# Gated two-layer transformer step on one core: register loads in batches, a twelve-place ring, later attention norms, and block results scaled on ScalarE

## The reference

```python
x = x + tanh(g_xattn[0]) * conv_mixer(layernorm(x), k, bias, ctx)      # filters over time, 8 heads
x = x + tanh(g_ffn[0])   * moe0(layernorm(x))                         # below
x = x + tanh(g_xattn[1]) * causal_attention(layernorm(x), ctx, ctx)   # 16 heads of 16 channels
x = x + tanh(g_ffn[1])   * lora_moe(layernorm(x))                     # 704 hidden, rank 16, 8 experts

def moe0(x):                                                          # E=8 experts, top 2, F=176
    probs = softmax(x @ Wr); w, sel = top_k(probs, 2)
    C = sum_k w[:, k] * one_hot(sel[:, k], E)
    routed = sum_e C[:, e] * ((silu(x @ Wg[e]) * (x @ Wu[e])) @ Wd[e])
    shared = (silu(x @ Sg) * (x @ Su)) @ Sd                           # 704 hidden
    return routed + sigmoid(x @ Wsg) * shared
```

## Time and profile before

| | us |
|---|---|
| median of 3 runs | 894.62 |
| lowest, highest | 890.34, 896.23 |
| the profiled execution, whole | 894.95 |
| its span, first to last instruction | 893.2 |

### The profile page before, as it was taken

How to read it: one execution, slowest core, us unless ns; L and a number is a source line. 1 busy time by engine, 2 the same in 40 slices (tenths; PEclk the granted TensorE clock), 3 DMA queues, 4 the chain that set the end, 5 groups by cost and what they waited for, 6 DMA issues and landing times.

```text
span 893.2 us, 13171 instructions
## 1 busy us (share of the span) xinstructions
PE 724.9 (81%) x4198; PEld 574.7 (64%) x4214; DVE 577.9 (65%) x1221; ACT 309.4 (35%) x539; POOL 256.0 (29%) x256
## 2 busy tenths in 40 slices
PE   2788888587978778877874888997769899999995
PEld 2565666476767656656662555665658788788884
DVE  5879888472356444444353778889457976877764
ACT  2110110154422222222232566875334335334231
POOL 1979777454447000000076810100100000000000
PEclk9999999797979899999995789998679999999997
DMA  8210100132213222222165512120010101001000
GB/s 271 71 50 27 36 24 1 48 95 74 70 56 140 67 78 68 73 73 77 42 110 98 81 50 82 54 85 2 1 47 1 48 25 48 1 24 48 23 1 24
DMA packets 42923, 51.25 MB, mean 57 GB/s; under 512 B 7088, under 2 KB 36976, under 8 KB 42224
## 3 DMA queue, kind: packets, MB, share of 16 engines
q1 hardware_dynamic: 36720, 41.98, 14.9%
q0 software_dynamic: 6144, 8.52, 4.8%
HBM read 36.88 MB, written 13.59 MB: 57 GB/s over the span
## 4 chain that ended last, share of the span: by engine, by line
PE 38%; DVE 16%; DMA 10%; issue 6%; POOL 5%; ACT 5%; SPq 2%; DVEq 0%; ACTq 0%; POOLq 0%
PE bank L2158 21%; DMA A<-x_d 4%; DMA X<-y_d,A 4%; PE bank L2009 3%; PE bank L1946 3%; POOL x_d L635 3%; DVE A L1505 3%; PE bank L2079 2%; DVE small L1495 2%; POOL X L641 2%; PE bank L2030 2%; ACT A L887 2%; PE bank L1996 1%; DMA A<-rows_d 1%; PE bank L2065 1%
## 5 line engine op out<-in xcount | busy, mean ns | idle before, releaser
L2158 PE MATMUL bank<-R 128*128 128x512 f32 (+3 forms) x1080 | 221.3, 365 | 22.4 <-DVE R L1617 6.4
L2158 PEld LDWEIGHTS bank<-R 128*128 128x128 f32 (+1 forms) x1080 | 183.2, 193 | 57.8 <-issue 8.3
L641 POOL DMA_INDIRECT X<-y_d,A x32 | 50.1, 1567 | 172.6 <-DMA y_d<-A 154.6
L1946 PE MATMUL bank<-R 128*128 128x512 f32 x264 | 74.4, 438 | 5.3 <-DVE R L1389 4.3
L1946 PEld LDWEIGHTS bank<-R 128*128 128x128 f32 x264 | 55.8, 218 | 17.5 <-issue 4.4
L2079 PE MATMUL bank<-ident,A 128*128 128x128 f32 x256 | 41.4, 314 | 30.4 <-ACT A L887 30.2
L2009 PE MATMUL bank<-R 128*128 x234 | 52.2, 362 | 13.4 <-issue 13.0
L1854 PE MATMUL bank<-A 128*128 128x256 f32 x128 | 43.2, 420 | 23.6 <-issue 12.4
L586 POOL TENSOR_TENSOR A<-A 128x256 f32<-128x256 f32 x64 | 58.0, 906 | 13.7 <-DVE A L1152 13.6
L2079 PEld LDWEIGHTS bank<-ident,A 128*128 128x128 f32 x256 | 33.4, 161 | 40.0 <-ACT A L887 25.4
L697 POOL TENSOR_TENSOR A<-A 128x512 f32<-128x512 f32 x4 | 5.2, 1288 | 180.1 <-DVE A L1611 180.1
(11 more groups left out here) (274 smaller groups left out, 1376.3 us busy)
## 6 DMA issues: line engine op xcount, KB each, us to landing
A<-x_d SPq DMA_DIRECT2D x39, 132.0 KB, 2.0
y_d<-A SPq DMA_DIRECT2D x39, 128.0 KB, 1.7
A<-rows_d SPq DMA_DIRECT2D x4, 1024.0 KB, 4.6
A<-in_w SPq DMA_DIRECT2D x8, 480.0 KB, 3.7
A<-in_w SPq DMA_DIRECT2D x5, 512.0 KB, 3.8
A<-in_ctx_one SPq DMA_DIRECT2D x8, 272.0 KB, 3.6
A<-in_ctx_half SPq DMA_DIRECT2D x8, 256.0 KB, 2.7
A<-in_ctx_nat SPq DMA_DIRECT2D x4, 512.0 KB, 3.7
```

Of the source, the lines that this page charges most:

```text
L641: nc.gpsimd.indirect_dma_start(out=X[:, b], out_offset=None, in_=y_d[:, :], in_offset=bass.IndirectOffsetOnAxis(ap=y_slots[:, b, r:r + 1], ...
L1946: mm = nc.tensor.matmul(dst, wX[:, a0:a0 + P], mX[:, k], start=(m == 0), stop=(m == 5))
L2158: mm = nc.tensor.matmul(dst, a, m, start=start and n == 0, stop=stop and n == len(prods) - 1, skip_group_check=skip)
```

## The change

Four things are changed.

1. **Registers.** The lists `t16` and `t256` go; `tcol` holds the plain expert. TensorE, ScalarE and SyncE each read all 39 numbers that they need with two instructions (20 and 19 numbers) ahead of the block loop and keep them in registers; the products with 16 and 256 are register steps ahead of the matmuls, as the addresses were before. The bounds assertions go.
2. **The ring.** `xb` has twelve places, at the start of the buffer (the rows' source, free once they are scattered), and loads run eight blocks ahead.
3. **`blk_out`** moves to ScalarE: a copy with the weight as a scale that is read per partition.
4. **Attention norms.** The norm of group g+1 is written in `c_steps(g)`, from step 2 for g=0 and from step 0 for g=1 and 2; before, group 1's stood ahead of the first reduce, group 2's in `c_steps(0)` and group 3's in `c_steps(1)`. ScalarE normalizes the rows of the next group in steps 3 to 6, not 0 to 3.

```diff
+REGS_PER_LOAD = 20
+XB = 12
+AHEAD = 8
+NORM_AT = (2, 0, 0)
...
-        xb = [A1[:, 11264 + i * XROW:11264 + (i + 1) * XROW] for i in range(6)]
+        xb = [A1[:, i * XROW:(i + 1) * XROW] for i in range(XB)]
...
+        def table_values(engine, view, top):
+            values = []
+            for lo in range(0, NBLK, REGS_PER_LOAD):
+                hi = min(lo + REGS_PER_LOAD, NBLK)
+                _, got = nc.values_load_multi_w_load_instructions(
+                    view[0:1, lo:hi], [engine], min_val=0, max_val=top,
+                    skip_runtime_bounds_check_because="the table's entries are bounded where it is made")
+                values.extend(got)
+            return values
...
 # SyncE
+            row_at = table_values(mybir.EngineType.SP, trow, X_ROWS - P)
             sp.wait_ge(rows_zeroed, 16 * (2 * E - 1))
             sp.wait_ge(rows_scattered, 16 * 2 * B)
             def block_in(i):
-                if i < 6:
-                    if i < 4:
-                        sp.wait_ge(xsL_ready, NCHUNK)
-                else:
-                    sp.wait_ge(y_made, i - 5)
-                at = sp.value_load(trow[0:1, i:i + 1], min_val=0, max_val=X_ROWS - P)
-                sp.dma_start(xb[i % 6], x_d[bass.ds(at, P), :]).then_inc(blk_loaded[i % 6], 16)
+                if i >= XB:
+                    sp.wait_ge(y_made, i - XB + 1)
+                sp.dma_start(xb[i % XB], x_d[bass.ds(row_at[i], P), :]).then_inc(blk_loaded[i % XB], 16)
...
 # ScalarE
+            def blk_out(i):
+                act.wait_ge(bdown_ready, i + 1)
+                if i >= 4:
+                    act.wait_ge(y_stored[i % 4], 16 * (i // 4))
+                weight = xb[i % XB][:, D:].rearrange("p (e n) -> p e n", n=1)[:, bass.ds(expert[i], 1), 0]
+                nc.scalar.activation(yo[i % 4], DB[i % 2][:, 0:D], ACT.Copy, scale=weight).then_inc(y_made, 1)
...
             act.wait_ge(down_done, 1 + SJ * PRE)
+            act.wait_ge(table_ready, 1)
+            expert.extend(table_values(mybir.EngineType.Activation, tcol, E - 1))
             blk_high_x(0)
-            for s in range(NBLK + 1):
+            for s in range(NBLK + 2):
                 if s + 1 < NBLK:
                     blk_high_x(s + 1)
                 if s < NBLK:
                     blk_silu(s)
-                if s >= 1:
+                if s >= 2:
+                    blk_out(s - 2)
+                if 1 <= s <= NBLK:
                     blk_high_h(s - 1)
...
-                    if more and k < BG:
-                        if k == 0:
+                    if more and 3 <= k < 3 + BG:
+                        if k == 3:
                             act.wait_ge(qT_turned, BG * (g + 1))
-                        c_norm_one(g + 1, k)
+                        c_norm_one(g + 1, k - 3)
...
 # VectorE: blk_out goes from its loop; the table
-                    step.mark(nc.vector.tensor_scalar(tcol, te_, float(D), None, ALU.add))
+                    nc.vector.tensor_copy(tcol, te_).then_inc(table_ready, 1)
...
-            def blk_out(i):
-                col = dve.value_load(tcol[0:1, i:i + 1], min_val=D, max_val=D + E - 1)
-                dve.wait_ge(bdown_ready, i + 1)
-                if i >= 4:
-                    dve.wait_ge(y_stored[i % 4], 16 * (i // 4))
-                nc.vector.tensor_scalar(yo[i % 4], DB[i % 2][:, 0:D], xb[i % 6][:, bass.ds(col, 1)], None, ALU.mult
-                                        ).then_inc(y_made, 1)
...
 # VectorE, c_steps(g, more)
-                if g + 2 < G:
-                    rows_complete(g + 2)
-                    norm = c_norm(BG * (g + 2), BG * (g + 3))
...
                 for k in range(8):
+                    if more and k == NORM_AT[g]:
+                        rows_complete(g + 1)
+                        norm = c_norm(BG * (g + 1), BG * (g + 2))
                     if k and (k < 6 or more):
                         c_shift(g + (k + 2) // 8, (k + 2) % 8, norm)
...
-                    norm.take(3 if more else 6)
+                    norm.take((3, 3, 8, 8)[k % 4] if more and g == 0 else 3 if more else 6)
+                    if more and k == 3:
+                        norm.take_all()
...
             nc.vector.memset(OT, 0.0).then_inc(ot_zeroed, 1)
-            rows_complete(1)
-            norm = c_norm(BG, 2 * BG)
-            norm.take(4)
             c_shift(0, 0)
-            norm.take(3)
-            c_shift(0, 1, norm)
-            c_shift(0, 2, norm)
-            norm.take_all()
+            c_shift(0, 1)
+            c_shift(0, 2)
...
 # TensorE
-                at = pe.value_load(t16[0:1, i:i + 1], min_val=0, max_val=(E - 1) * RANK)
...
-                                              w[:, k, :, :, bass.ds(at, RANK)], start=(m == 0), stop=(m == 5))
+                                              w[:, k, :, :, bass.ds(expert[i] * RANK, RANK)], start=(m == 0), stop=(m == 5))
...
-                at = pe.value_load(t256[0:1, i:i + 1], min_val=0, max_val=(E - 1) * D)
...
             def blocks():
                 pe.wait_ge(table_ready, 1)
+                pe.wait_ge(xsL_ready, NCHUNK)
+                expert.extend(table_values(mybir.EngineType.PE, tcol, E - 1))
```

42 lines of the change are left out of this document (19 added, 23 removed).

## The result

The changed kernel takes 859.14 us (median of 4 runs, 854.64 to 861.37); the kernel before took 892.94 us in its 4 runs on the same chip. The ratio is 0.9613, with a 95% interval of 0.9557 to 0.9669: 3.9% faster. The profiled execution took 857.65 us with a span of 855.9 us, 37.3 us less than the 893.2 us before.

A forecast was written before the change was run, and what follows sets the result against it. The block loop was taken as bound by a chain of row loads, register loads and results, and attention's start by a gather wait. 894.95 - 31.5 - 8.2 - 0.7 + 0.4 = 855 us, range 841 to 872.

The forecast's parts named there:

- The loop, -31.5 forecast: Block loop: 35 blocks fall from 3.67 to 2.77 us each, saving 31.5 us.
- The ring was worked out at 2.69 us: Block loop: down matmuls, ScalarE's result, high half, VectorE's low half, next down; 2.69 us, longer than TensorE's 2.5, so it decides.
- rival (3): TensorE alone sets the loop's pace at 2.5 us, ScalarE's work fits beside it, third norm hidden; 841.3 us, chance 0.13.
- Step (a): Block loop: the row load's 2.02 us leaves the chain, being issued six turns ahead instead of two.
- Rival (1): Block loop: register loads were already hidden, only the landing goes, 3.2 us per block; 870 us, chance 0.17.
- 0 and -0.7 forecast: Before the loop: bulk register loads hidden, costing 0; SyncE's first row load starts 0.7 us sooner.
- rival (2): At the loop's door: registers load one after another at 0.27 us each, 7.4 us visible; 862.4 us, chance 0.15.
- Step (d): Attention start: the first reduce starts when scores end, without waiting for group 1's rows and statistics; 11.0 us saved.
- (e): Attention, between third and fourth reduce: the wait behind group 1's norm, a gather and group 2's statistics goes; 1.4 us saved.
- Step (f): Attention: the third group of steps, which had no norm, now carries one; costs 4.2 us.
- Rival (4): Denser loop drops TensorE's clock to its lower level through half of attention; 930 us, slower than before, chance 0.03.
- late keys: Attention: the 34 us groups growing to 38 would mean that SyncE's next keys come late.

The follow-up runs named there:

- kernel 9: Changed kernel with ScalarE making the next block's high half before it scales the earlier block's result, not after; 839.88 us, ratio 0.9419.
- kernel 6: Changed kernel with each block's result scaled on VectorE again, its registers loaded in bulk there; 848.64 us, ratio 0.9506.
- kernel 12: Changed kernel with the ring of six, four rows ahead, and each block's result on VectorE; 865.25 us, ratio 0.9699.
- kernel 3: Changed kernel with two norms in the first eight attention steps, the fourth in the second eight, ScalarE's normalisations four steps before the turn; 846.25 us, ratio 0.9466.
- kernel 2: Kernel before the change with only the attention part of the change; 891.01 us, ratio 0.998.
- kernel 8: kernel 3 with ScalarE's normalisations back in steps 3 to 6; 849.01 us, ratio 0.9498.
- kernel 1: Changed kernel with the attention part put back as before; 854.02 us, ratio 0.9545.
- kernel 7: kernel 3 with SyncE loading eight registers first, then one per row, ScalarE one per result, TensorE 20 before the loop and 19 after the second turn; 847.07 us.
- kernel 10: Changed kernel with the norms ahead as in kernel 3 and each block's result on VectorE as in kernel 6; 833.92 us, ratio 0.9351.

## Why the prediction was right, and where its terms were off

The time was forecast at 855 us and measured at 859 (857.65 in the profiled execution), by terms that were partly wrong in both directions: the loop gave 9.3 us more than forecast, the start of the loop 4.6 and attention 6.5 us less. That the mechanism of the loop was seen is no luck; that these errors nearly cancel is.

**The loop, -31.5 forecast, -40.8 measured.** That ScalarE's result stands in a ring with the high half, the low half and the next down group, and that this ring and not TensorE alone decides, is what kernel 9 shows. The ring was worked out at 2.69 us and is 2.49: ScalarE's next operation starts 0.38 us after the result starts, not 0.49 + 0.03, and the other three steps are 0.06 shorter together. The 3% added for slow landings and the lower clock didn't come; the clock was 1.00 throughout. The result itself was taken at 0.49 and took 0.474. TensorE alone was put at 2.5 and is at most 2.26 (kernels 6 and 9). So rival (3)'s pace of 2.5 came, by the forecast's mechanism.

**The load of rows and the registers.** Step (a), the landing leaves the chain, holds; with the old ring it stays in it (kernel 12, 2.81 us). Rival (1), by which these loads were hidden and only the landing mattered, fails. The prediction gave the loads no price of their own beside (a), which takes the whole ring of before away at once. The bulk loads alone are worth 29.9 of the 49.4 us that lie between the old loop and the best one.

**Around the loop, 0 and -0.7 forecast, +3.9 measured.** The step that failed is "at 0.27 us an instruction that is 0.5, hidden". A bulk load's price is one for each register, as rival (2) had it: 4.1 to 5.3 us an instruction. Rival (2) looked at TensorE alone; SyncE and ScalarE load their registers too, and SyncE's first row load went out at 292.47, where it was 289.91 before, and not 0.7 us sooner. The Trainium skill's figure (Runtime: NRT & Kernel Launch, Instruction fetch mechanics), about 200 ns a register in bulk, is near the 0.22 to 0.25 us here, though that page speaks of loads from HBM and these read a table that VectorE had made in on-chip memory; the 4.7 us that the prediction worked out from it stand against 3.9.

**Attention, -8.2 forecast, -1.7 measured.** Step (d) was -11.0 and is -12.1; (e) was -1.4 and is -2.4. Step (f) failed: +4.2 forecast, +12.8 measured. The windows of the earlier trace rows were cut unevenly, but that mattered little: by eights of eight intervals each, 38.0, 33.5 and 31.4 us, a norm costs 6.6 or 2.1, 4.4 in the mean. What failed is that the step asked how much work a norm adds and not what stands behind it. A norm that is made in the group of steps which wants it puts ScalarE's normalisation right ahead of the turn of the queries, and that step's transposes are queued behind the turn; a norm made a group ahead does not. With the norms ahead (kernel 3) the steps take 106.9 us, 4.0 more than before, which is about the price that (f) put on the work alone. The other 8.8 us are these waits and the lower clock that comes with them in this execution: in the third eight, the one that can be compared at one clock, 4.0 and 2.5 us (kernels 2, 3 and 8). No engine was overloaded: in the last 16 intervals TensorE was busy for 63.9 of 74.7 us.

**The rest.** Rival (4), a lower clock from a denser loop, fails: the loop's clock rose from 0.97 to 1.00. The clock did fall in attention, to 0.91 in the second and third eight, but kernels 1 and 3 have as dense a loop and 1.00 and 0.97 there. That the third group of eight steps would take near 34 us was wrong (38.0), and not by late keys.

**Open.** How the cost of the norms splits between VectorE and ScalarE in the first and second eight; what lowers the clock there; how short the loop would be if TensorE alone held it; and why the time behind the last reduce is 266.5 to 267.2 us in kernels 3, 7, 9 and 10 and 269.3 to 273.2 in the others, with the same code.

## What to carry to other kernels

A chain that names one engine only doesn't show that this engine sets the pace: look on the timeline at what ended just before each of its groups starts, and whether the distance is the same in every turn, and try the order of two operations on the engine next to it before moving one elsewhere. In an in-order queue the place of a short operation can cost although its engine is far from full: the loop's result (0.47 us) cost 0.25 us a block on a ScalarE that was busy for 46.9 of 87.6 us, and nothing one place later (kernel 9 against kernel 6); the norms cost 12.8 us in one place and 4.0 in another. Ask who is queued behind it. A register load in bulk is little cheaper per register than a single one; what it buys is that its time leaves the loop, and it is paid at the door by every engine that does it.

## What the runs showed of the hardware

A load of 20 registers in one instruction takes 4.46 us (ScalarE), 4.82 (SyncE) or 5.30 (TensorE), one of 19 takes 4.06 to 4.52, so 0.21 to 0.27 us for each register; a single one takes 0.27 to 0.30, and 0.38 on ScalarE between other work (kernel 7). TensorE's weight load starts 0.15 us after the end of the VectorE operation that releases it, in each of 35 blocks of four kernels. ScalarE started an operation 0.38 us after the start of one that is shown with 0.47 us, so neighbours on that engine overlap by 0.09 us. TensorE's group of six down matmuls takes 0.99 us from its first start to its last end (medians of 35) in the kernel before and in the changed kernel, where its first weight load had stood still for some 0.33 and 0.36 us, 0.97 in kernel 9 (0.11) and 0.87 in kernel 12 (0.14), with the same operands. The chain shows 0.72 for kernel 12, since it leaves out 0.16 us in which the group overlaps with the one before it. Why the group is 0.1 us shorter in kernel 12 no run tested.
